# Graph layer on one Trainium2 core: the difference x[src] − x[dst] formed by an adding gather instead of a VectorE subtraction

## The chip, the cores and the metric

One core of a Trainium2 chip runs the whole program. The metric is the device time of one execution in microseconds (us); lower is better. Before the change it is 1676.12 us, the median of 3 runs (1675.56 to 1676.58).

## What is computed

`x` has 50000 rows of 512 float32. `src` and `dst` list 62500 edges, sorted by `dst`: 50000 self loops and 12500 others. Cut to what matters:

```python
msg  = x[src]
agg  = segment_sum(msg, dst, n)
deg  = segment_sum(ones, dst, n)
mean = agg / maximum(deg, 1)[:, None]
h    = mean @ W_l + b + x @ W_r
out  = layernorm(x + h * sigmoid(h))
```

Every node has its self loop, so the kernel writes mean as x[node] plus a correction, the sum of (x[src] − x[dst]) over the other edges of that node, divided by its degree. Then h = x @ (W_l + W_r) + b + correction @ W_l, and a correction is needed only for nodes that have edges other than the loop.

## The kernel before, in words

All products are float32 made of three float32r products (`three`, L484 to L491): a high and a low part of each factor, 12 matmuls of 128x512 for one tile of 128 rows. The five engine programs are written out by hand; each runs its own list of steps in order, and semaphores join them. There are three stages.

*Early stage (to about 171 us).* 44 early tiles of 128 node rows are transposed, split and multiplied by W_l + W_r; the products go to DRAM. POOL makes the low part of each early tile (`split_early`, L369 to L376), ACT the high part, a copy and the product's copy (`round_early`, `keep_early`, L629 to L641). Beside it VectorE sorts the 12500 edges out of the list (bitwise moves on `Z`, `cor`, `w_sum`) and finds node positions. Its last piece, `loop_cols` (L818 to L821), has nine rounds; `single(0, scan)` (L942) stands between round six and round seven. `upto` (L945), which PE waits for before the first edge tile, comes after round nine.

*Edge stage (173 to 527 us).* 98 tiles of 128 edges. For edge tile t:

- POOL gathers 128 rows of x by `dst` (`gather_xd`, L396) and by `src` (`gather_xs`, L400), each one indirect DMA of 256 KB, into rings of four buffers, `xd` and `xs`.
- VectorE subtracts (`subtract`, L892 to L899) into one of two `diff` buffers.
- PE turns the difference with four transposes into a PSUM buffer (`turn`, L551 to L557).
- VectorE makes running sums along equal `dst` with four scans (`scan`, L901 to L914); ACT takes the high part (`round_sums`, L660), VectorE the low part (`split_sums`, L920), PE multiplies by W_l with `three`, and VectorE scales and adds the bias (`finish`, L926). SP stores the tile as correction rows and loads `join_row`, which says where a run of equal `dst` goes on.

Orders in this stage: VectorE does, at step t, finish(t−1), scan(t+1), subtract(t+2), split_sums(t+1). PE does turn(t+1), then the 12 matmuls of tile t. ACT does round_sums(t+1). POOL issues xd(t), then xs(t); it runs ahead until the ring is full, since xd(t) waits for subtract(t−4).

Before the stage, POOL issues the gathers of tiles 0 to 3 between the early tiles 32 to 39, VectorE subtracts tiles 0 and 1 (L937, L938), and PE turns tile 0 ahead of early tile 40 (L560).

*Node stage (from 528 us).* 174 pairs of node tiles: 8 transposes, 24 matmuls, correction rows gathered and added, silu, residual, normalisation, store. The 44 early tiles are finished beside it ("light").

Of the kernel before, what the change touches and what calls it, by code (L numbers as in the profile page):

```python
# [6 lines left out]
def gnn_layer(nc, x, src, dst, w_l, w_r, bias, out):  # L7
    f32, f32r, i32 = mybir.dt.float32, mybir.dt.float32r, mybir.dt.int32
    ALU = mybir.AluOpType
    ACT = mybir.ActivationFunctionType  # L10
    P = nc.NUM_PARTITIONS

    N, D = x.shape
# [11 lines left out]
    ET = -(-R // P)  # L25
# [3 lines left out]
    EARLY = 44  # L29
    BASE = EARLY * P  # L30
    NP = -(-(NTILES - EARLY) // 2)
    MERGE_ROUND, FIND_ROUND = 4, 8
# [10 lines left out]
    with ctx:  # L43
        def sb(name, shape, dt):
            return ctx.enter_context(nc.sbuf_tensor(name, shape, dt))

        def sem(name):
            return ctx.enter_context(nc.semaphore(name))
# [3 lines left out]
        eye = eye3[:, P:2 * P]  # L52
# [30 lines left out]
        dst_idx, src_idx = sb("dst_idx", [P, ET], i32), sb("src_idx", [P, ET], i32)  # L83
        dst_f = sb("dst_f", [P, 1 + ET], f32)
        rdeg = sb("rdeg", [P, ET], f32)
        xs = [sb(f"xs{b}", [P, D], f32) for b in range(4)]
        xd = [sb(f"xd{b}", [P, D], f32) for b in range(4)]
        diff = [sb(f"diff{b}", [P, D], f32) for b in range(2)]
        join_row = sb("join_row", [P, 4, P], f32)
        sums = sb("sums", [P, 2, K, P], f32)  # L90
        s_hi = [sb(f"s_hi{b}", [P, K, P], f32r) for b in range(2)]
# [34 lines left out]
        pT = [ctx.enter_context(nc.psum_tensor(f"pT{b}", [P, 2, D], f32)) for b in range(2)]  # L126
# [26 lines left out]
        xs_in = [sem(f"xs_in{b}") for b in range(4)]  # L153
        xd_in = [sem(f"xd_in{b}") for b in range(4)]
        list_made, list_stored = sem("list_made"), sem("list_stored")
        row_in = [sem(f"row_in{b}") for b in range(4)]
        diff_made = sem("diff_made")
        turned, sums_made, s_hi_made, s_lo_made, c_product, c_made = (sem("turned"), sem("sums_made"),
                                                                     sem("s_hi_made"), sem("s_lo_made"),
                                                                     sem("c_product"), sem("c_made"))  # L160
# [25 lines left out]
        def fixed(v):  # L186
            return isinstance(v, int)

        def wait(eng, s, v):

            if not fixed(v) or v > 0:
                eng.wait_ge(s, v)
# [9 lines left out]
        def peeled(first, end, step):  # L202
            for t in range(first, end):
                step(t, t // 4, t % 4)
# [16 lines left out]
        def shifted(t, q, u, by, n, step):  # L221

            if not fixed(t) or 0 <= t + by < n:
                step(t + by, q + (u + by) // 4, (u + by) % 4)

        def single(t, step):
            step(t, t // 4, t % 4)

        def ring(q, u, n):

            return u % n, q * (4 // n) + u // n
# [120 lines left out]
        def _(pool):  # L352
            g = nc.gpsimd
# [36 lines left out]
            def gather(out_, table, idx, rows, bound, s):  # L390
                g.indirect_dma_start(out=out_, out_offset=None, in_=table,  # L391
                                     in_offset=bass.IndirectOffsetOnAxis(ap=idx, axis=0),
                                     bounds_check=bound, oob_is_err=False).then_inc(s, 16)


            def gather_xd(t, q, u):  # L396
                wait(pool, diff_made, t - 3)
                gather(xd[u][:], x, dst_idx[:, t:t + 1], P, N - 1, xd_in[u])

            def gather_xs(t, q, u):  # L400
                gather(xs[u][:], x, src_idx[:, t:t + 1], P, N - 1, xs_in[u])

            pool.wait_ge(dst_found, 1)
            for e in range(4):
                single(4 * FIND_ROUND + 2 * e, split_early)
                single(e, gather_xd)
                single(4 * FIND_ROUND + 2 * e + 1, split_early)
                single(e, gather_xs)
            peeled(4 * FIND_ROUND + 8, EARLY, split_early)
            for t in range(4, ET):  # L410
                single(t, gather_xd)
                single(t, gather_xs)

            for b in range(2):
                pool.wait_ge(c_stored[b], 16 * (ET // 2))
# [64 lines left out]
        def _(pe):  # L480
# [3 lines left out]
            def three(ps, hi, lo, w_hi, w_lo, arriving=None):  # L484

                terms = [(a, w, k) for k in range(K) for a, w in ((hi, w_hi), (hi, w_lo), (lo, w_hi))]
                for n, (a, w, k) in enumerate(terms):
                    if arriving and n % 3 == 0:
                        pe.wait_ge(arriving, k + 1)
                    last = mm(ps, a[:, k], w[:, k], start=(n == 0), stop=(n == len(terms) - 1))  # L490
                return last  # L491
# [58 lines left out]

            def turn(t, q, u):  # L551
                b = u % 2
                wait(pe, diff_made, t + 1)
                wait(pe, sums_made, t - 1)
                for k in range(K):
                    last = nc.tensor.transpose(pT[b][:, 1, k * P:(k + 1) * P], diff[b][:, k * P:(k + 1) * P], eye)
                last.then_inc(turned, 1)  # L557


            single(0, turn)  # L560
            peeled(4 * FIND_ROUND + 8, EARLY, early_tile)
            pe.wait_ge(rdeg_ready, 1)
            pe.wait_ge(upto_ready, 1)
            mm(before_ps, eye3[:, P - 1:2 * P - 1], upto[:, 1:1 + NTILES], start=True, stop=False)
# [16 lines left out]
                last.then_inc(transposed, 1)  # L581

            def edge_tile(t, q, u):
                shifted(t, q, u, 1, ET, turn)
                if fixed(t) and t == ET - 1:
                    single(0, transpose_x)
                b = u % 2
                wait(pe, s_hi_made, t + 1)
                wait(pe, s_lo_made, t + 1)
                wait(pe, c_made, t - 1)  # L590
                three(pH[b][:, 0, :], s_hi[b], s_lo[b], wl_hi, wl_lo).then_inc(c_product, 1)
            steps(pe, ET, edge_tile)


# [19 lines left out]
        def _(act):  # L614
            a_ = nc.scalar.activation
# [53 lines left out]
            def reset_light(l):  # L669
                wait(act, light_z, l)  # L670
                a_(l_cor[:], bias_rows[:], ACT.Copy).then_inc(light_reset, 1)

            peeled(EARLY - 4, EARLY, early_tile)
            single(0, round_sums)
            single(EARLY - 1, keep_early)
            act.wait_ge(bias_in, 16)
# [1 line left out]

            def edge_tile(t, q, u):
                shifted(t, q, u, 1, ET, round_sums)  # L680
                if fixed(t) and t == ET - 5:
                    act.wait_ge(idx_ready, 1)
                    reset_light(0)
                    single(0, reset_cor)
                    single(1, reset_cor)
            steps(act, ET, edge_tile)


# [58 lines left out]
        def _(dve):  # L747
            v = nc.vector
# [140 lines left out]
            dve.wait_ge(bias_in, 16)  # L889


            def subtract(t, q, u):  # L892

                b = u % 2
                r, used = ring(q, u, 4)
                dve.wait_ge(xs_in[r], 16 * (used + 1))
                dve.wait_ge(xd_in[r], 16 * (used + 1))
                wait(dve, turned, t - 1)
                v.tensor_tensor(diff[b][:], xs[r][:], xd[r][:], ALU.subtract).then_inc(diff_made, 1)  # L899

            def scan(t, q, u):  # L901

                b = u % 2
                r, used = ring(q, u, 4)
                dve.wait_ge(row_in[r], 16 * (used + 1))
                wait(dve, turned, t + 1)
                wait(dve, sums_made, t)
                wait(dve, s_lo_made, t - 1)
                wait(dve, s_hi_made, t - 1)
                for k in range(K):  # L910
                    last = v.tensor_tensor_scan(  # L911
                        sums[:, b, k], join_row[:, r], pT[b][:, 1, k * P:(k + 1) * P],
                        0.0 if fixed(t) and t == 0 else sums[:, 1 - b, k, P - 1:P], ALU.mult, ALU.add)
                last.then_inc(sums_made, 1)  # L914
# [14 lines left out]
            def find_nodes():  # L929
                dve.wait_ge(before_ready, 1)  # L930
                then(v.tensor_tensor(none, upto[:, 1:1 + NTILES], before_ps, ALU.subtract))
                then(v.tensor_scalar(none, none, 0.0, float(SKIP), ALU.is_equal, ALU.mult))
                v.memset(node_idx[:, NTILES:NTILES + 1], SKIP)
                v.scalar_tensor_tensor(node_idx[:, 0:NTILES], upto[:, 1:1 + NTILES], -1.0, none, ALU.add, ALU.add
                                       ).then_inc(idx_ready, 1)

            single(0, subtract)  # L937
            single(1, subtract)  # L938
            dve.wait_ge(loops_merged, 1)
            then(v.tensor_copy(loop_col[0], pH[1][:, 0]))  # L940
            loop_cols(0, col_bits - 3)
# [4 lines left out]
            single(0, split_sums)  # L946

            def edge_tile(t, q, u):
                shifted(t, q, u, -1, ET, finish)
                shifted(t, q, u, 1, ET, scan)  # L950
                shifted(t, q, u, 2, ET, subtract)
                shifted(t, q, u, 1, ET, split_sums)
                if fixed(t) and t == 2:
                    find_nodes()
            steps(dve, ET, edge_tile)


# [121 lines left out]
```

## Time and profile before

| | |
|---|---|
| median of 3 runs | 1676.12 us |
| the profiled execution | 1675.46 us |
| its span, first to last instruction | 1673.6 us |
| mean granted clock of TensorE | 0.993 of full |
| PE busy | 1607.3 us, 96% |
| VectorE (DVE) busy | 1446.7 us, 86% |
| ACT busy | 972.1 us, 58% |
| POOL busy | 1014.5 us, 61% |
| chain that ended last | issue 30%, PE 20%, POOL 19%, DVE 17%, ACT 10% |

Times in the rows count from the start of the span. "Idle before" is the time in which the engine did nothing ahead of an instruction, and the name behind the arrow is what ended it. Matmul ends are modelled, so PE's busy time overlaps and says less than the distance between two starts. DMA share is the mean busy share of 16 DMA engines.

### The profile page before, as it was taken

To read this page: it belongs to the slowest core of one execution; us is meant where nothing else is said; L and a number is where in the kernel's file an instruction comes from. 1 tells how busy PE (TensorE), PEld (TensorE's weight loads), DVE (VectorE), ACT (ScalarE), POOL (GpSimd) and SP (SyncE) were. 2 spreads that over 40 slices of the span, in tenths; PEclk is the share of its full clock that TensorE was granted. 3 is DMA by queue.
4 is the path that set the end of the run, shared out by engine and by line. 5 is a ranking of instruction groups with operands and counts; after the bars stand their busy time and mean duration, and the time that the engine had idled before them with its cause. 6 is when DMAs were issued, how large, how long until landed. Compare 5 with 4: busy or idle time off the path is not lost.

```text
span 1673.6 us, 30193 instructions
## 1 busy us (share of the span) xinstructions
PE 1607.3 (96%) x7886; PEld 1315.8 (79%) x7886; DVE 1446.7 (86%) x2468; ACT 972.1 (58%) x1237; POOL 1014.5 (61%) x1306
## 2 busy tenths in 40 slices
PE   7998999999999999999999999999999999999995
PEld 5887777777777788888878888887888888888884
DVE  8889999999997788888888888888888888888886
ACT  4443111111113677777767777776777777777775
POOL 5445555555553666666666666665666666666664
PEclk9999999999999999999999999999999999999998
DMA  5455788888885566666666666766666666666664
GB/s 181 150 163 173 211 238 235 238 235 236 238 233 176 159 211 224 207 218 212 211 206 217 206 223 202 224 206 200 226 198 228 203 223 211 216 207 213 209 218 162
DMA packets 204143, 349.25 MB, mean 209 GB/s; under 512 B 37020, under 2 KB 51126, under 8 KB 204117
## 3 DMA queue, kind: packets, MB, share of 16 engines
q1 hardware_dynamic: 156135, 274.22, 49.4%
q0 software_dynamic: 46944, 74.22, 17.1%
q10 hardware_dynamic: 1038, 0.50, 0.1%
q8 instruction: 11, 0.18, 0.0%
q14 instruction: 15, 0.12, 0.0%
HBM read 288.78 MB, written 139.67 MB: 256 GB/s over the span
## 4 chain that ended last, share of the span: by engine, by line
issue 30%; PE 20%; POOL 19%; DVE 17%; ACT 10%; POOLq 2%; DVEq 1%; DMA 1%; ACTq 0%; SPq 0%
PE pH L490 17%; POOL cor L391 6%; ACT O L703 4%; DVE Z L975 4%; DVE stats L990 3%; POOL rstd L462 3%; POOL light_cor L391 3%; ACT cor L666 2%; DVE sums L911 2%; POOL l_var_eps L442 2%; POOL var_eps L459 2%; ACT light_o L720 2%; DVE l_stats L1017 2%; POOL l_rstd L444 1%; ACT s_hi L660 1%
## 5 line engine op out<-in xcount | busy, mean ns | idle before, releaser
L490 PE MATMUL pH<-ws_hi,x_hi 128*128 128x512 f32 x1564 | 631.5, 404 | 13.6 <-DVE x_lo L962 6.7
L490 PE MATMUL pH<-ws_hi,x_lo 128*128 128x512 f32 x1564 | 613.3, 392 | 0.0
L490 PE MATMUL pH<-ws_lo,x_hi 128*128 128x512 f32 x1564 | 611.1, 391 | 0.0
L391 POOL DMA_INDIRECT cor<-correction_rows,node_now x347 | 370.8, 1069 | 215.4 <-POOL node_now L423 148.4
L490 PEld LDWEIGHTS pH<-ws_hi,x_hi 128*128 128x128 f32 x1564 | 295.1, 189 | 77.4 <-issue 22.7
L490 PEld LDWEIGHTS pH<-ws_hi,x_lo 128*128 128x128 f32 x1564 | 294.5, 188 | 64.5
L711 ACT ACTIVATE Z<-Z 128x1024 f32<-128x1024 f32 x174 | 184.2, 1058 | 272.2 <-DVE Z L975 236.0
L490 PEld LDWEIGHTS pH<-ws_lo,x_hi 128*128 128x128 f32 x1564 | 295.9, 189 | 55.2
L703 ACT ACTIVATE O<-Z,shift,rstd 128x512 f32<-128x512 f32 x347 | 261.5, 801 | 3.7 <-DVE shift L1001 3.7
L975 DVE TENSOR_TENSOR Z<-pH,cor 128x1024 f32<-128x1024 f32 x174 | 212.0, 1218 | 27.3 <-issue 15.2
L660 ACT ACTIVATE s_hi<-sums 128x512 fp32r<-128x512 f32 x98 | 62.0, 632 | 287.8 <-DVE sums L911 177.4
L990 DVE BATCH_NORM_STATS2 stats<-Z 128x6 f32<-128x512 f32 x347 | 221.5, 680 | 0.0
L982 DVE TENSOR_TENSOR Z<-Z,X 128x1024 f32<-128x1024 f32 x174 | 213.2, 1225 | 0.0
L962 DVE TENSOR_TENSOR x_lo<-pT,x_hi 128x1024 fp32r<-128x1024 f32 x174 | 207.3, 1191 | 2.2 <-ACT x_hi L694 2.0
L694 ACT ACTIVATE x_hi<-pT 128x1024 fp32r<-128x1024 f32 x174 | 175.2, 1007 | 36.0 <-PE pT L579 21.6
L666 ACT ACTIVATE cor<-bias_rows 128x1024 f32<-128x1024 f32 x174 | 181.5, 1044 | 0.0
L579 PEld LDWEIGHTS pT<-eye,X 128*128 128x128 f32 (+1 forms) x1388 | 161.0, 140 | 24.7 <-DMA X<-in_x 2.7
L579 PE MATMUL pT<-eye,X 128*128 128x128 f32 (+1 forms) x1388 | 179.8, 272 | 0.5 <-DMA X<-in_x 0.5
L462 POOL TENSOR_TENSOR rstd<-var_eps,minus_half 128x2 f32<-128x2 f32 x174 | 171.2, 984 | 14.5
L490 PE MATMUL pH<-wl_hi,s_hi 128*128 128x512 f32 x392 | 161.8, 413 | 15.3 <-DVE s_lo L920 5.2
L391 POOL DMA_INDIRECT xd<-in_x,dst_idx x98 | 99.3, 1014 | 122.1 <-DVE diff L899 119.5
L911 DVE TENSOR_TENSOR_SCAN sums<-join_row,sums,pT 128x128 f32<-128x128 f32 x388 | 153.8, 458 | 1.6 <-issue 1.6
(131 smaller groups left out, 1789.7 us busy)
## 6 DMA issues: line engine op xcount, KB each, us to landing
X<-in_x SPq DMA_DIRECT2D x173, 512.0 KB
out<-O SPq DMA_DIRECT2D x173, 512.0 KB
correction_rows<-c_out SPq DMA_DIRECT2D x98, 256.0 KB
light_x<-in_x SPq DMA_DIRECT2D x66, 256.0 KB
light_h<-early_product SPq DMA_DIRECT2D x44, 256.0 KB
out<-light_o SPq DMA_DIRECT2D x44, 256.0 KB
join_row<-joined SPq DMA_DIRECT2D x98, 64.0 KB
light_h<-in_x SPq DMA_DIRECT2D x22, 256.0 KB, 2.7
```

The source lines that it names most:

```text
L391: g.indirect_dma_start(out=out_, out_offset=None, in_=table, in_offset=bass.IndirectOffsetOnAxis(ap=idx, axis=0), bounds_check=bound, oob_ ...
L462: g.tensor_tensor(rstd[0:rows, b, 0:nt], var_eps[0:rows, b, 0:nt], minus_half[0:rows, 0:nt], ALU.pow).then_inc(rstd_made, 1)
L490: last = mm(ps, a[:, k], w[:, k], start=(n == 0), stop=(n == len(terms) - 1))
L579: last = nc.tensor.transpose(pT[u % 2][:, a, k * P:k * P + rows], X[0:rows, b, a, k * P:(k + 1) * P], eye[0:rows, 0:rows])
L666: a_(cor[u][:], bias_rows[:].rearrange("p (a n) -> p a n", a=1).to_broadcast([P, 2, D]), ACT.Copy).then_inc(cor_reset, 1)
L703: last = a_(O[0:rows, b, a], Z[0:rows, u % 4, a], ACT.Identity, scale=rstd[0:rows, b, a:a + 1], bias=shift[0:rows, b, a:a + 1])
L711: a_(Z[0:rows, b, 0:nt], Z[0:rows, b, 0:nt], ACT.Silu).then_inc(silu_made, 1)
L911: last = v.tensor_tensor_scan(sums[:, b, k], join_row[:, r], pT[b][:, 1, k * P:(k + 1) * P], 0.0 if fixed(t) and t == 0 else sums[:, 1 - b ...
L962: v.tensor_tensor(x_lo[b][:, 0:nt, :, 0:rows], pT[b][:, 0:nt].rearrange("p a (k r) -> p a k r", k=K)[:, :, :, 0:rows], x_hi[b][:, 0:nt, :, ...
L975: v.tensor_tensor(Z[0:rows, b, 0:nt], pH[u % 2][0:rows, 0:nt], cor[b][0:rows, 0:nt], ALU.add).then_inc(z_made, 1)
L982: v.tensor_tensor(Z[0:rows, b, 0:nt], Z[0:rows, b, 0:nt], X[0:rows, b, 0:nt], ALU.add).then_inc(u_made, 1)
L990: v.bn_stats(stats[0:rows, u % 2, a], Z[0:rows, u % 4, a]).then_inc(stats_made, 1)
```

## The change

The subtraction leaves VectorE. The gather of x[dst] goes straight into `diff`, now four buffers; ACT turns its sign in place (`negate`, Copy with scale −1); then the gather of x[src] is an indirect DMA that adds onto the same buffer. `xs` and `xd` are gone. Each adding gather waits for the sign of its tile. In POOL's list xs(t−1) now comes after xd(t), and xs(0) to xs(3) have moved behind the early tiles 40 to 43; xd(t) waits for turn(t−4). PE turns two tiles ahead of the product instead of one, waits for the adding gather to land, and turns tile 0 only after early tile 42 and tile 1 after early tile 43. VectorE does scan(t+1), finish(t−1), split_sums(t+1).

```diff
-        xs = [sb(f"xs{b}", [P, D], f32) for b in range(4)]
-        xd = [sb(f"xd{b}", [P, D], f32) for b in range(4)]
-        diff = [sb(f"diff{b}", [P, D], f32) for b in range(2)]
+        diff = [sb(f"diff{b}", [P, D], f32) for b in range(4)]
...
             def gather_xd(t, q, u):
-                wait(pool, diff_made, t - 3)
-                gather(xd[u][:], x, dst_idx[:, t:t + 1], P, N - 1, xd_in[u])
+                wait(pool, turned, t - 3)
+                gather(diff[u][:], x, dst_idx[:, t:t + 1], P, N - 1, xd_in[u])
             def gather_xs(t, q, u):
-                gather(xs[u][:], x, src_idx[:, t:t + 1], P, N - 1, xs_in[u])
+                wait(pool, negated, t + 1)
+                g.indirect_dma_start(out=diff[u][:], out_offset=None, in_=x,
+                                     in_offset=bass.IndirectOffsetOnAxis(ap=src_idx[:, t:t + 1], axis=0),
+                                     bounds_check=N - 1, compute_op=ALU.add).then_inc(xs_in[u], 16)
             for e in range(4):
                 single(4 * FIND_ROUND + 2 * e, split_early)
                 single(e, gather_xd)
                 single(4 * FIND_ROUND + 2 * e + 1, split_early)
+            for e in range(4):
+                single(4 * FIND_ROUND + 8 + e, split_early)
                 single(e, gather_xs)
-            peeled(4 * FIND_ROUND + 8, EARLY, split_early)
             for t in range(4, ET):
                 single(t, gather_xd)
-                single(t, gather_xs)
+                if t > 4:
+                    single(t - 1, gather_xs)
+            single(ET - 1, gather_xs)
...
             def turn(t, q, u):
                 b = u % 2
-                wait(pe, diff_made, t + 1)
+                r, used = ring(q, u, 4)
+                pe.wait_ge(xs_in[r], 16 * (used + 1))
                 wait(pe, sums_made, t - 1)
...
+            peeled(4 * FIND_ROUND + 8, EARLY - 1, early_tile)
             single(0, turn)
-            peeled(4 * FIND_ROUND + 8, EARLY, early_tile)
+            single(EARLY - 1, early_tile)
+            single(1, turn)
...
             def edge_tile(t, q, u):
-                shifted(t, q, u, 1, ET, turn)
+                shifted(t, q, u, 2, ET, turn)
...
-            peeled(EARLY - 4, EARLY, early_tile)
+            def negate(t, q, u):
+                act.wait_ge(xd_in[u], 16 * (ring(q, u, 4)[1] + 1))
+                a_(diff[u][:], diff[u][:], ACT.Copy, scale=-1.0).then_inc(negated, 1)
+
+            for e in range(4):
+                single(EARLY - 4 + e, early_tile)
+                single(e, negate)
...
                 shifted(t, q, u, 1, ET, round_sums)
+                shifted(t, q, u, 4, ET, negate)
...
-                v.tensor_tensor(diff[b][:], xs[r][:], xd[r][:], ALU.subtract).then_inc(diff_made, 1)
...
-            single(0, subtract)
-            single(1, subtract)
...
             def edge_tile(t, q, u):
+                shifted(t, q, u, 1, ET, scan)
                 shifted(t, q, u, -1, ET, finish)
-                shifted(t, q, u, 1, ET, scan)
-                shifted(t, q, u, 2, ET, subtract)
                 shifted(t, q, u, 1, ET, split_sums)
```

## Rows read from the trace of the kernel before

**Rows 1.** Busy time by stretch: start and end, length, then engines, clock, DMA share, GB/s.

```profile
200.00:500.00 300.00, 286.21 (x1331) 222.07 (x1330) 287.61 (x583) 52.51 (x83) 166.57 (x167) 1.00 0.84 236
700.00:1100.00 400.00, 396.41 (x1980) 329.84 (x1980) 342.90 (x574) 297.64 (x358) 261.56 (x371) 1.00 0.66 212
```

**Rows 2.** Groups of instructions in the edge stage, 200 to 500 us.

```profile
L490 PE MATMUL pH<-wl_hi,s_hi 128*128 128x512 f32 x333 | 137.5, 413 | 13.9 <-DVE s_lo L920 5.0 <-issue 4.5
L911 DVE TENSOR_TENSOR_SCAN sums<-join_row,sums,pT 128x128 f32<-128x128 f32 x333 | 132.0, 458 | 0.0
...
L391 POOL DMA_INDIRECT xd<-in_x,dst_idx x84 | 83.8, 997 | 107.6 <-DVE diff L899 106.1 <-issue 1.5
L391 POOL DMA_INDIRECT xs<-in_x,src_idx x83 | 83.4, 1005 | 27.1 <-issue 25.0 <-DVE diff L899 2.1
L926 DVE SCALAR_TENSOR_TENSOR c_out<-pH,rdeg,bias_rows 128x512 f32<-128x512 f32 x84 | 62.7, 746 | 1.2
...
L920 DVE TENSOR_TENSOR s_lo<-sums,s_hi 128x512 fp32r<-128x512 f32 x83 | 57.4, 692 | 11.2 <-ACT s_hi L660 3.9 <-issue 0.2
L899 DVE TENSOR_TENSOR diff<-xs,xd 128x512 f32<-128x512 f32 x83 | 55.3, 666 | 0.0
L660 ACT ACTIVATE s_hi<-sums 128x512 fp32r<-128x512 f32 x83 | 52.5, 633 | 247.2 <-DVE sums L911 145.6 <-issue 101.6
```

**Rows 3.** Timeline, one edge tile: start, length, engine, line.

```profile
303.49 0.69 DVE L920 TENSOR_TENSOR s_lo<-sums,s_hi 128x512 fp32r<-128x512 f32 x1
...
304.41 0.50 PE L490 MATMUL pH<-wl_hi,s_hi 128*128 128x512 f32 x1 [0.25 <-DVE s_lo L920]
```

**Rows 4.** Timeline, first matmul of edge tile 0 and of edge tile 97.

```profile
173.35 0.47 PE L490 MATMUL pH<-wl_hi,s_hi 128*128 128x512 f32 x1
...
524.31 0.47 PE L490 MATMUL pH<-wl_hi,s_hi 128*128 128x512 f32 x1
```

**Rows 5.** Groups of PE in the node stage, 700 to 1100 us.

```profile
L490 PE MATMUL pH<-ws_hi,x_hi 128*128 128x512 f32 x495 | 198.3, 401 | 3.6 <-issue 2.4
...
L579 PE MATMUL pT<-eye,X 128*128 128x128 f32 x496 | 64.3, 272 | 0.0
```

**Rows 6.** DMA queues in the edge stage, 200 to 500 us: packets, MB, share of 16 engines.

```profile
q0 software_dynamic: 13290, 43.57, 58.1%
q1 hardware_dynamic: 23931, 27.22, 26.0%
```

**Rows 7.** DMA issues: KB each and median us from issue to landing.

```profile
light_h<-in_x SPq DMA_DIRECT2D x22, 256.0 KB, 2.7
bias_rows<-in_L_gnn_b SPq DMA_DIRECT2D x1, 256.0 KB, 6.4
```

**Rows 8.** Timeline, end of the early stage and start of the edge stage.

```profile
156.00 0.60 PE L556 MATMUL pT<-eye,diff 128*128 128x128 f32 x4
...
162.34 1.35 DVE L911 TENSOR_TENSOR_SCAN sums<-join_row,pT 128x128 f32<-128x128 f32 x4
...
163.28 0.60 ACT L641 ACTIVATE light_u<-pH 128x512 f32<-128x512 f32 x1
163.47 1.30 POOL L375 TENSOR_TENSOR x_lo<-light_cor,x_hi 128x512 fp32r<-128x512 f32 x1 [3.66 <-ACT light_cor L635]
...
165.22 0.48 PE L490 MATMUL pH<-ws_hi,x_hi 128*128 128x512 f32 x1
...
167.85 0.39 PE L490 MATMUL pH<-ws_hi,x_lo 128*128 128x512 f32 x1
168.20 0.47 PE L490 MATMUL pH<-ws_hi,x_hi 128*128 128x512 f32 x1
...
171.10 0.36 DVE L945 CAST O<-Z 128x391 f32<-128x391 int32 x1
```

**Rows 9.** Busy time by stretch, the start of the node stage, columns as in rows 1.

```profile
546.00:556.00 10.00, 7.54 (x42) 6.21 (x40) 4.42 (x9) 2.91 (x5) 6.92 (x10) 1.00 0.26 78
556.00:566.00 10.00, 8.56 (x35) 6.92 (x36) 7.50 (x12) 6.24 (x9) 7.61 (x11) 0.83 0.55 181
```

More of the change, by code:

```diff
@@ L156, in gnn_layer @@
         row_in = [sem(f"row_in{b}") for b in range(4)]
-        diff_made = sem("diff_made")
+        negated = sem("negated")
         turned, sums_made, s_hi_made, s_lo_made, c_product, c_made = (sem("turned"), sem("sums_made"),
@@ L407, in _ @@
                 single(4 * FIND_ROUND + 2 * e + 1, split_early)
+            for e in range(4):
+                single(4 * FIND_ROUND + 8 + e, split_early)
                 single(e, gather_xs)
-            peeled(4 * FIND_ROUND + 8, EARLY, split_early)
+            assert EARLY == 4 * FIND_ROUND + 12
             for t in range(4, ET):
                 single(t, gather_xd)
-                single(t, gather_xs)
+                if t > 4:
+                    single(t - 1, gather_xs)
+            single(ET - 1, gather_xs)
             for b in range(2):
@@ L552, in turn @@
                 b = u % 2
-                wait(pe, diff_made, t + 1)
+                r, used = ring(q, u, 4)
+                pe.wait_ge(xs_in[r], 16 * (used + 1))
                 wait(pe, sums_made, t - 1)
                 for k in range(K):
-                    last = nc.tensor.transpose(pT[b][:, 1, k * P:(k + 1) * P], diff[b][:, k * P:(k + 1) * P], eye)
+                    last = nc.tensor.transpose(pT[b][:, 1, k * P:(k + 1) * P], diff[r][:, k * P:(k + 1) * P], eye)
                 last.then_inc(turned, 1)
+            peeled(4 * FIND_ROUND + 8, EARLY - 1, early_tile)
             single(0, turn)
-            peeled(4 * FIND_ROUND + 8, EARLY, early_tile)
+            single(EARLY - 1, early_tile)
+            single(1, turn)
             pe.wait_ge(rdeg_ready, 1)
@@ L889, in _ @@
             dve.wait_ge(bias_in, 16)
[L892 to L898, printed above, removed]
-                v.tensor_tensor(diff[b][:], xs[r][:], xd[r][:], ALU.subtract).then_inc(diff_made, 1)
             def scan(t, q, u):
```

## The prediction

> **What bounds the kernel now.** I read busy time by stretch first. In the edge stage VectorE is busy 287.6 of 300 us, PE 286.2 [rows 1]; both look full, so the groups decide. The 83 low parts in that window count 83 tiles. VectorE has 287.61 / 83 = 3.47 us of work a tile, of which the subtraction is 0.67 us, and nearly no idle time: the low part's 11.2 us in all is its largest [rows 2]. PE's busy time overlaps, so I compare spacings instead. From tile 0 to tile 97 there are 97 steps in 524.31 − 173.35 us [rows 4], 3.62 us each. In the node stage PE is busy 396 of 400 us [rows 1] and does 496 / 8 = 62 pairs [rows 5], 6.45 us a pair. A pair is 24 matmuls and 8 transposes; an edge tile asks for 12 and 4, exactly half, 3.23 us. So PE could run this loop at 3.23 and runs at 3.62; in the timeline it starts a tile when the low part has ended [rows 3]. VectorE bounds the edge stage, by its sum of work. ACT works 52.5 of 300 us there; POOL's 107.6 us before xd are waits for the subtraction [rows 2].
>
> **Removed.** 98 subtractions of 0.67 us. VectorE's work falls from 3.47 to 2.80 us a tile. PE is late next: 3.23. The scans, low part and `finish` keep their waits; since `finish` now stands between scan and low part, the 0.63 us of ACT's high part falls beside its 0.75 us [rows 2].
>
> **Signs on ACT.** 98 Copies of the high part's size, 0.63 us each [rows 2]. ACT's work becomes 1.27 us of 3.23, hidden in time in which it waits for VectorE. Behind a late sign the next high part would queue, and VectorE's low part behind that.
>
> **POOL's queue.** Two issues a tile stay, 1.00 us each with 0.33 us (27.1 / 83) between [rows 2]: 2.66 us a tile. What an adding gather costs POOL no row shows. Lower bound: the plain gather, 1.00, or a little less, which would gain nothing as POOL is then not late. Upper: two plain gathers, 2.01, as it reads two operands; that gives 3.67. Up to 1.56 is hidden under PE's 3.23. I take 1.3: nearer to one plain gather, as the list of rows is the same and written once. xd(t+2) now queues behind xs(t), so behind a sign; the ring of four gives it two steps, 6.5 us, against about 3 us until it is issued and 2.7 us to land (an estimate from a direct 256 KB load, rows 7).
>
> **The adding gather's landing.** PE reads tile t two steps after ACT's sign. The sign ends about 1.5 us into its step (two ACT instructions and their waits, an estimate from 2 × 0.63), so 2 × 3.23 − 1.5 = 5.0 us remain for issue and landing. The direct load lands in 2.7 us at the median, one at the start of the kernel took 6.4 [rows 7]. Taking 2.7 plus the 1.3 of POOL: hidden. If it is late, the turn holds up on PE the 12 matmuls queued behind it, two tiles older, and VectorE's `finish` waits for those. At 6.4 the loop would be bound by it at (1.5 + 6.4) / 2 = 3.95 us.
>
> **The DMA engines.** The queue of the gathers held them 58.1% of 300 us for 167 gathers: 1.04 us each; the other queue 26.0%, 0.94 us a tile [rows 6]. A tile takes 3.03 us of them. An adding gather has to read its target as well. Lower bound, as a plain one: 3.03. Upper, twice a plain one: 4.07. Which is nearer? The other queue moved 27.22 MB in 78 us, at which 262 KB take 0.75 us; a gather takes 1.04, just POOL's issue time, so I infer that part of it is waiting for POOL's list, which shrinks once the queue is never empty. Then the tile needs 0.75 + 1.50 + 0.94 = 3.19 us. I take this; it is so close to 3.23 that I put the loop at 3.25. **Loop: 97 × (3.62 − 3.25) = 35.9 us saved.**
>
> The Trainium skill, "Collectives: The Full Stack", section on the bandwidth ceiling, says that an add made in the DMA engine is slow not through the add but because two sources are read through the same ring, so half the rate. No run here shows it yet. By that rule the tile needs 4.07 us of the engines, and the sum would come out slower; it is the second rival.
>
> **The start.** Tile 0 is turned at 156.00 today and scanned at 162.34 [rows 8]; nothing waits there. After the change xs(1) waits for the sign of tile 1, which ACT makes after the copy at 163.28: 163.28 + 0.60 + 0.63 = 164.5. POOL issues it (1.3) and then splits early tile 42, 1.30 us, done by 167.1; today that split starts at 163.47. PE's early tile 42 starts at 167.2 instead of 165.22, takes 168.20 − 165.22 = 2.98, and turn(0) ends about 0.6 later, at 170.7. The scan of tile 0 moves from 162.34 to 170.7: **8.4 us**, and with it the three rounds behind it, `upto` (171.10, rows 8) and every edge tile, since VectorE stands still meanwhile. Lower bound: 168.20 − 162.34 = 5.9, if the splits are not late; upper 10.4, if each adding gather holds POOL 0.7 us longer three times over. PE then idles some 6 us before edge tile 0. After a similar lull in the node stage the granted clock was 0.83 in a 10 us stretch [rows 9], 1.7 us lost, so one spell at 1.2 GHz: I add 1.5, between 0 and 1.7. The two first subtractions leave 1.3 us earlier; I count nothing, they are far ahead of this wait.
>
> **Sum.** −35.9 + 8.4 + 1.5 = −26.0 on the profiled execution's 1675.46, so 1649.5; the median stands 0.66 above it: **1650 us**. Everything after 528 us is unchanged. Break-even is a loop of 3.62 − 9.9 / 97 = 3.52 us. About 0.2% (3.4 us) is what a measurement of this kernel can tell from no change.
>
> **The rivals.**
>
> 1. *POOL becomes the bound.* An adding gather of 2.01 us gives 3.67 us a tile, +4.9, with the start +9.9 and about 2 more for three longer issues: 1693, slower. It decides from 1.86 us of issue (1.66 + 1.86 = 3.52). For: two reads to describe for each row. Against: POOL's 1.00 us is steady for one list of 128 rows [rows 2].
> 2. *The DMA engines become the bound.* At 4.07 us a tile: 97 × 0.45 = +43.7, with the start +53.6: 1730, slower. It decides from 1.54 us of engine time per adding gather (3.52 − 1.04 − 0.94). A landing of 6.4 us ends near it, at 1718. For: the engines are 84% busy already [rows 1], and the add needs one more read. Against: the waiting share of a gather's 1.04 us.
> 3. *Half of it.* The adding gather costs 1.5 us of the engines and nothing shrinks: 3.48 us, 13.6 saved against 9.9: 1672, within 0.2% or just beyond.
> 4. *VectorE does not get faster.* The loop stays at 3.62 because a chain, not the sum, holds it: 1686. Against: low parts waited for ACT 3.9 us in 300 [rows 2].
>
> **How the numbers follow.** Forecast (loop 3.19 to 3.45) 0.50; rival 3 near zero 0.08; rival 1 with 4 0.17; rival 2 and beyond 0.25. Faster 0.50, same 0.08, slower 0.42. The forecast's own range is 1643 (loop 3.19, the start at 8.4 alone) to 1669 (3.45, the start at 9.9). The range of all reaches to rival 2: 1643 to 1730, leaving out landings or reads still slower (0.13) and a loop under 3.19 (0.03).
>
> **What would show it.** Right: the first matmuls of tiles 0 and 97 some 315 us apart; VectorE below 90% busy in that stretch and waiting for PE; `negate` at 0.63 us; POOL idle before xs for ACT and not the other way; scan(0) near 170.7 with VectorE idle ahead of it; node stage as before. Wrong: POOL's adding DMA_INDIRECT over 1.86 us with no idle time (rival 1); turns that wait on the DMA, with the gather queue's share over 70% (rival 2); spacing at 3.62 with VectorE idle before the low part (rival 4). The forecast falls if the step from tile to tile is above 3.52 us, whatever the start costs.

## The result, and the profile after

The changed kernel takes 1745.65 us (median of 4 runs, 1742.88 to 1750.02) against 1675.84 us for the kernel before: a ratio of 1.0418, 95% interval 1.0403 to 1.0433. It is slower by 4.2%. The prediction was 1650 us; its range of 1643 to 1730 does not reach the measured time. Its rival 2 had the direction right, at 1730, for another reason.

Nearly the whole difference lies in the edge stage and its start. Busy time by stretch of the changed kernel, the edge stage and a stretch of the node stage (columns as in rows 1: length, then PE, its weight loads, VectorE, ACT and POOL, then the clock and the DMA):

```profile
200.00:500.00 300.00, 239.15 (x1117) 183.53 (x1117) 202.04 (x419) 86.81 (x139) 182.05 (x140) 0.98 0.84 198
...
800.00:1200.00 400.00, 394.97 (x1976) 329.13 (x1975) 341.82 (x571) 296.64 (x357) 263.16 (x369) 1.00 0.65 213
```

Against [rows 1], PE fell from 286 to 239 us of 300 and VectorE from 288 to 202. No engine is full any more. The node stage is as it was. The timeline of the changed kernel: the scan of tile 0, then the first matmul of tiles 0 and 97, which answer to [rows 4, 8].

```profile
171.83 1.35 DVE L918 TENSOR_TENSOR_SCAN sums<-join_row,pT 128x128 f32<-128x128 f32 x4 [8.98 <-PE pT L563]
...
182.41 0.78 PE L496 MATMUL pH<-wl_hi,s_hi 128*128 128x512 f32 x1
...
596.29 0.48 PE L496 MATMUL pH<-wl_hi,s_hi 128*128 128x512 f32 x1
```

Tile 0 starts 182.41 − 173.35 = 9.1 us later. (In the other runs below that keep this start it lies between 180.37 and 182.71, so this term is good to 2 us.) The 97 steps take 413.9 us, 4.27 us each instead of 3.62: 62.9 us more. Together that is 72.0 of the 72.7 us by which the span grew (1746.3 against 1673.6). The groups of the edge stage say who waits (200 to 500 us, columns as in rows 2):

```profile
L400 POOL DMA_INDIRECT diff<-in_x,src_idx x70 | 107.9, 1542 | 97.2 <-ACT diff L684 87.5 <-issue 9.7
L389 POOL DMA_INDIRECT diff<-in_x,dst_idx x70 | 74.1, 1059 | 21.3 <-issue 20.7 <-PE pT L563 0.6
...
L563 PE MATMUL pT<-eye,diff 128*128 128x128 f32 x280 | 45.6, 286 | 60.8 <-DMA diff<-in_x,src_idx 60.7
...
L684 ACT ACTIVATE diff<-diff 128x512 f32<-128x512 f32 x69 | 43.5, 630 | 99.3 <-DMA diff<-in_x,dst_idx 96.2 <-issue 3.0
```

It is a circle of waits: PE's turn waits for the adding gather to land, POOL's adding gather for ACT's sign, the sign for the plain gather (xd) to land. And xd hardly waits at all: POOL issues it as soon as the adding gather ahead of it is out. The chain of waits, followed back from the last instruction and at each step to what released it, shows the circle closing. Here is one lap, and the signs that begin the next ones (start, length, what; a DMA row counts from the start of POOL's issue to the landing):

```profile
251.27 0.64 ACT diff L684
...
252.69 1.53 POOL diff L400
254.23 0.30 issue
254.53 4.62 DMA diff<-in_x,dst_idx
259.15 0.45 issue
259.60 0.64 ACT diff L684
...
267.75 0.64 ACT diff L684
...
276.33 0.64 ACT diff L684
...
285.42 0.64 ACT diff L684
```

Sign of tile t (0.64), hand-over to POOL (0.8), adding gather xs(t) (1.53), gap (0.30), then xd(t+2), which stands behind xs(t) in POOL's list and lands 4.6 us after its issue began, then the sign of tile t+2. That is 259.60 − 251.27 = 8.3 us for two tiles. The four laps from 251.27 to 285.42 take 8.2 to 9.1 us, 8.54 on average, and half of that is 4.27, the spacing measured. The landing of xd is 50.6% of the chain from 250 to 330 us, in pieces of 4.2 to 5.8 us. In between, the chain leaves the circle: from 286.85 it runs through an adding gather's landing (6.41), the turn and a product.

### The profile page after: what moved, and what is told of

It reads as the page before. It is cut to its first block, busy times and chain, and to the rows that moved or that the text cites. A ratio compares the mean times of both kernels' runs of the same rounds, so it can differ in the third digit from the quotient of the medians.

```text
span 1746.3 us, 30033 instructions
## 1 busy us (share of the span) xinstructions
PE 1609.2 (92%) x7886; PEld 1316.2 (75%) x7886; DVE 1389.8 (80%) x2370; ACT 1032.6 (59%) x1335; POOL 1073.4 (61%) x1306
## 4 chain that ended last, share of the span: by engine, by line
issue 29%; POOL 22%; DMA 14%; DVE 11%; PE 11%; ACT 10%; POOLq 2%; DVEq 1%; SPq 0%; ACTq 0%
DMA diff<-in_x,dst_idx 11%; PE pH L496 9%; POOL cor L389 6%; ACT O L719 4%; DVE Z L979 4%; POOL diff L400 3%; DVE stats L994 3%; POOL rstd L468 3%; POOL light_cor L389 2%; POOL l_var_eps L448 2%; DMA diff<-in_x,src_idx 2%; ACT cor L675 2%; POOL var_eps L465 2%; ACT light_o L736 2%; DVE l_stats L1021 2%
## 5 line engine op out<-in xcount | busy, mean ns | idle before, releaser
L400 POOL DMA_INDIRECT diff<-in_x,src_idx x98 | 151.7, 1548 | 144.1 <-ACT diff L684 121.5
```

The costliest lines, as they stand in the source:

```text
L400: g.indirect_dma_start(out=diff[u][:], out_offset=None, in_=x, in_offset=bass.IndirectOffsetOnAxis(ap=src_idx[:, t:t + 1], axis=0), bounds ...
```

## The experiments

Two theories stood first. **A:** POOL's list closes a lap of latencies over two tiles. **B:** the DMA engines are the bound, as rival 2 had it; for B spoke the DMA queues of the changed kernel in the edge stage (packets, MB, share of 16 engines), 84% in sum as in [rows 6], but for 70 tiles instead of 83:

```profile
q0 software_dynamic: 15642, 36.63, 61.1%
q1 hardware_dynamic: 20047, 22.74, 23.0%
```

Spacing below is always (first matmul of tile 97 − first matmul of tile 0) / 97, from the timeline of the run.

**One place further back in POOL's list (e2_queue3).**

```diff
-                if t > 4:
-                    single(t - 1, gather_xs)
+                if t > 5:
+                    single(t - 2, gather_xs)
```

> One line changed against the changed kernel: POOL issues xs(t-2) behind xd(t) instead of xs(t-1). Nothing else, same bytes, same adding gather. Theory A (POOL's queue closes a lap: xd(t+2) stands behind xs(t), which waits for the sign of tile t, which waits for xd(t) to land; in the chain of waits about 5.0 landing + 0.64 sign + 0.6 + 1.54 adding issue + 0.30 = 8.1 to 8.6 us for two tiles): the lap now spans three tiles, 2.8 us a tile, and the next one holds: sign, adding issue and its landing of about 5.4 us have two steps, (1.5 + 0.6 + 5.4) / 2 = 3.75 us a tile, so about 97 x 0.5 = 50 us less than the changed kernel's 1746: 1685 to 1710. Theory B (the 16 DMA engines are the bound; the adding gather takes 1.77 us of them, a tile 3.58 us at 84% busy): the order changes nothing, 1740 to 1750.

Measured: 1730.87 us, ratio 1.0313 (1.0295 to 1.0330), spacing 4.08 us. The order matters, so pure B fails, but A's price missed by 21 us. (B's 1.77 us for an adding gather is more than the rows above give: 0.611 × 300 / 70 = 2.6 us for both gathers of a tile, less 1.0 for the plain one.) The chain of waits of this run shows another lap:

```profile
260.10 0.67 PE pT L564 x4
...
261.54 1.02 POOL diff L389
262.56 0.30 issue
262.87 5.52 DMA diff<-in_x,src_idx
...
268.50 0.67 PE pT L564 x4
```

Now the adding gather of tile t−2 stands behind xd(t), which waits for the turn of tile t−4. From turn to turn it is 8.4 us, again for two tiles.

**The same, with the sign five tiles ahead (e3_queue3_sign5)** (`shifted(t, q, u, 5, ET, negate)`, and the sign of tile 4 ahead of the loop).

> As e2_queue3, and ACT turns the sign five tiles ahead instead of four. Theory A: the sign's chain has three steps now, and what is left is one lap of the ring of four: turn, xd issued and landed (5.0), sign, another xd issue in POOL (1.3), adding issue and landing (5.4), 13.8 us in all for four tiles, 3.45 us a tile, so about 80 us less than the changed kernel: 1655 to 1690. Theory B: 1740 to 1750 as before.

Measured: 1731.45 us, ratio 1.0320 (1.0294 to 1.0345), spacing 4.07. A miss by 41 us: I had counted ACT's place and overlooked the second lap, which does not go through the sign at all.

**Eight buffers, three places back (e4_ring8).**

```diff
-        diff = [sb(f"diff{b}", [P, D], f32) for b in range(4)]
+        diff = [sb(f"diff{b}", [P, D], f32) for b in range(8)]
...
-                wait(pool, turned, t - 3)
+                wait(pool, turned, t - 7)
...
-                if t > 4:
-                    single(t - 1, gather_xs)
+                if t > 6:
+                    single(t - 3, gather_xs)
...
-                shifted(t, q, u, 4, ET, negate)
+                ahead(t, q, u, 6, ET, negate)
```

(PE and ACT loop over eight tiles a turn for it; `ahead` is `shifted` for that loop; the signs of tiles 4 and 5 stand ahead of the loop.)

> Ring of eight diff buffers instead of four (PE's and ACT's loops unrolled by eight for it), POOL issues xs(t-3) behind xd(t), ACT turns the sign six tiles ahead. No latency chain is left that spans fewer than three tiles. Theory A: the loop falls to what the engines can do, PE 3.23 us a tile, the DMA engines between 3.2 and 3.5: 1650 to 1675, the start still about 9 us later than before. Theory B: 1735 to 1750, with the DMA share of the edge stage at 0.84 or more and a tile still above 4.1 us.

Measured: 1648.12 us, ratio 0.9826 (0.9810 to 0.9843). That is 2 us under A's range, and B is out. The first matmuls of tiles 0 and 97, from its timeline:

```profile
180.37 0.48 PE L511 MATMUL pH<-wl_hi,s_hi 128*128 128x512 f32 x1
...
494.20 0.48 PE L511 MATMUL pH<-wl_hi,s_hi 128*128 128x512 f32 x1
```

That is 3.235 us a tile, PE's half of a node pair (3.23) to the hundredth. From 250 to 300 us its chain of waits is PE alone (from 300 to 440 us it also runs through landings, VectorE and POOL), and its queues carry the same adding gathers at that pace:

```profile
249.95 2.75 PE pH L511 x12
252.70 0.44 PE pT L577 x4
253.14 2.75 PE pH L511 x12
```

```profile
q0 software_dynamic: 19610, 45.61, 69.0%
q1 hardware_dynamic: 27471, 32.61, 31.8%
```

The shares add up to 101%, and PE waits for landings less than 1 us of the 300. So a share near 100% does not show that the DMA engines hold the loop. POOL is another matter:

```profile
L414 POOL DMA_INDIRECT diff<-in_x,src_idx x88 | 136.3, 1549 | 28.1 <-issue 26.2 <-ACT diff L698 1.9
L403 POOL DMA_INDIRECT diff<-in_x,dst_idx x85 | 90.4, 1063 | 25.9 <-issue 11.9 <-ACT diff L698 11.0 <-PE pT L577 3.0
```

Two issues and two gaps of about 0.3 us are 1.55 + 1.06 + 0.6 = 3.2 us a tile. POOL's list is as full as PE's, and no run separates the two bounds.

**Eight buffers, and the start put back (e5_ring8_start).** Signs and adding gathers of tiles 0 to 3 go between early tiles 36 and 41, tile 0 is turned ahead of early tile 40 again. PE's part of the edit, against e4_ring8:

```diff
+            turn(0, 0, 0)
-            peeled(4 * FIND_ROUND + 8, EARLY - 1, early_tile)
-            turn(0, 0, 0)
-            single(EARLY - 1, early_tile)
+            peeled(4 * FIND_ROUND + 8, EARLY, early_tile)
             turn(1, 0, 1)
```

> As e4_ring8, and the start put back: signs and adding gathers of tiles 0 to 3 between early tiles 36 and 41, tile 0 turned ahead of early tile 40 as in the kernel before. Theory A with the start's price of 9.1 us (first matmul of tile 0 at 182.41 instead of 173.35): 8 to 10 us below e4_ring8, 1640 to 1666, so below the kernel before. If the start costs nothing in the end (something later absorbs it): the same time as e4_ring8. Theory B: about 1737.

Measured: 1642.67 us, ratio 0.9789 (0.9773 to 0.9806), the fastest of all. Its tile 0 starts here, at 174.40 instead of 180.37:

```profile
174.40 0.48 PE L511 MATMUL pH<-wl_hi,s_hi 128*128 128x512 f32 x1
```

The start gave 6.0 us at tile 0 in the trace and 5.5 in the medians, less than the 8 to 10 expected: tile 0 of e4_ring8 had already started 2.0 us ahead of the changed kernel's, and here it still starts 1.05 us behind the kernel before.

**Is it the ring or the order (e6_ring8_near)?** The two laps can be written down. With n buffers and xs(t) standing d places behind, xd(t+d+1) waits behind xs(t): a lap of d+1 tiles. And xs(t) waits behind xd(t+d), which waits for the turn of tile t+d−n: a lap of n−d tiles. With n = 4 one of them always spans two tiles, for d = 1 as for d = 2. This is theory A2. Eight buffers with d = 1 (`t - 1` again):

> As e4_ring8 (eight buffers, 3.24 us a tile), but POOL issues xs(t-1) behind xd(t) again, as the changed kernel does. Theory A2 (two laps through POOL's list: xd(t+d+1) stands behind xs(t), d+1 tiles a lap; xs(t) stands behind xd(t+d), which waits for turn(t+d-n), n-d tiles a lap; each lap is some 8.1 to 8.6 us; with d = 1 the first spans two tiles whatever the ring): about 4.1 to 4.3 us a tile, 1730 to 1750, as if the ring were still four. Rival C (it is the number of buffers that counts, or the loops unrolled by eight): 1645 to 1652 as e4_ring8.

Measured: 1778.63 us, ratio 1.0590 (1.0563 to 1.0616), spacing 4.61. C is out: eight buffers alone gain nothing. But 29 us over the range needs a reason. The groups show it:

```profile
L943 DVE TENSOR_TENSOR s_lo<-sums,s_hi 128x512 fp32r<-128x512 f32 x65 | 45.0, 692 | 108.2 <-ACT s_hi L683 107.0
```

In the changed kernel this row waits for nothing (0.0 us). Here ACT waits 222.1 of 300 us at signs six tiles ahead whose gathers have not landed, and the high part queues behind them. To test that, the same kernel with the sign four ahead (e9_ring8_near_sign4; the signs of tiles 4 and 5 ahead of the loop go too):

```diff
-                ahead(t, q, u, 6, ET, negate)
+                ahead(t, q, u, 4, ET, negate)
```

> As e6_ring8_near (eight buffers, xs(t-1) behind xd(t)), with ACT turning the sign four tiles ahead as in the changed kernel, instead of six. Against the changed kernel only the ring and the loops unrolled by eight differ. e6_ring8_near took 4.61 us a tile, more than the 4.3 expected, with VectorE's low part waiting 107 of 300 us for ACT's high part, which stands behind a sign that waits for its gather. Theory A2 (the lap through POOL's list spans two tiles whatever the ring, and the excess in e6_ring8_near is ACT's line behind the early sign): 4.2 to 4.3 us a tile as in the changed kernel, 1738 to 1752. If the excess comes from eight buffers or from the unrolled loops: 1770 to 1785 again. If the ring is what counted: under 1700.

Measured: 1747.19 us, ratio 1.0436 (1.0418 to 1.0454), spacing 4.25, the changed kernel's 4.27 with eight buffers. VectorE's low part waits for nothing again:

```profile
L941 DVE TENSOR_TENSOR s_lo<-sums,s_hi 128x512 fp32r<-128x512 f32 x71 | 48.4, 682 | 0.0
```

Buffers and unrolled loops are worth nothing while d is 1.

**Two places back with eight buffers (e7_ring8_mid)** (laps of three and six tiles).

> As e4_ring8, with xs(t-2) behind xd(t). Theory A2: laps of three and of six tiles, 8.4 / 3 = 2.8 us, so PE still holds the loop at 3.24: 1645 to 1652. If the lap in this setting is longer because landings are (5.6 us instead of 5.0 in e4_ring8), 9.2 / 3 = 3.07, still under 3.24. Rival C: the same time; rival D (the lap grows with every tile of distance lost): 1690 or so.

Measured: 1651.91 us, ratio 0.9850 (0.9834 to 0.9867), spacing 3.27. The time is at the upper end of A2's range. But from 250 to 300 us the chain of waits runs through landings and POOL's issues and not through PE, and ACT waits 172.5 us for landings, against 14.8 in e4_ring8: the laps priced at 2.8 to 3.1 us a tile seem to leave little in reserve.

**The sign taken out of the lap (e8_no_sign).** POOL waits for xd's landing itself (the four signs ahead of the loop go too):

```diff
-                wait(pool, negated, t + 1)
+                pool.wait_ge(xd_in[u], 16 * (ring(q, u, 4)[1] + 1))
...
-                shifted(t, q, u, 4, ET, negate)
```

> The changed kernel without the sign: ACT's negate is left out and POOL's adding gather waits for the landing of xd itself, so the output is made of x[src] + x[dst]. Same order, ring and adding gather. Theory A2: the lap loses the sign's 0.64 us and one hand-over of about 0.5 us, 8.5 - 1.2 = 7.3 us for two tiles, 3.65 a tile, so 97 x 0.6 = 58 below the changed kernel: 1680 to 1700. Theory B (the DMA engines' capacity): the same DMA work, 1740 to 1750.

Measured: 1720.66 us (2 runs), ratio 1.0260 (1.0233 to 1.0287), spacing 4.00. Faster than the changed kernel by 25 us with the same DMA work, so it is a latency; but 21 us above the range. One lap of its chain:

```profile
253.39 1.54 POOL diff L400
254.93 0.30 issue
255.23 5.49 DMA diff<-in_x,dst_idx
...
261.50 1.54 POOL diff L400
```

From 255.23 + 5.49 to 261.50 POOL's hand-over still takes 0.8 us: 1.54 + 0.30 + 5.49 + 0.8 = 8.1 for two tiles, 4.05 a tile. The sign's 0.64 us is gone, but the hand-over of 0.5 that the expectation took off is not, and the landings in this stretch of the chain, to 300 us, are 5.4 us and more.

**The adding taken out (e1_plain_second).**

```diff
-                                     bounds_check=N - 1, compute_op=ALU.add).then_inc(xs_in[u], 16)
+                                     bounds_check=N - 1).then_inc(xs_in[u], 16)
```

> The changed kernel with a plain second gather, which overwrites where the other adds, so x[dst] is left out of the result. Same order, waits, ring and sign. Theory A2: the lap loses 0.54 us of POOL's issue (1.54 to 1.00) and perhaps 0.5 to 0.9 us of xd's landing, which queues behind the adding gather: 7.1 to 7.8 us for two tiles, 3.55 to 3.9 a tile, 1680 to 1710: most of the loss stays without any adding. If the adding in the DMA engines is the cause: 3.24 to 3.4 a tile and 1650 to 1665.

Measured: 1707.33 us (2 runs), ratio 1.0181 (1.0160 to 1.0201), spacing 3.82. POOL's second issue is back to 1.04 us:

```profile
L400 POOL DMA_INDIRECT diff<-in_x,src_idx x78 | 81.3, 1042 | 110.0 <-ACT diff L684 71.9 <-issue 19.8 <-PE pT L563 18.4
```

With two plain gathers and the same order the kernel is still 30 us slower than the kernel before. Against PE's 3.24 the changed kernel loses 1.03 us a tile; 0.58 of it stays without any adding, and 0.45 goes with it. The split of the 0.45 is an estimate: 0.50 us a lap is the longer issue, and the landings of xd on the chain of waits from 200 to 475 us average 5.2 us in the changed kernel (27 of them) and 4.7 here (20).

## Why the prediction was wrong, point by point

- *What bounds the kernel now; VectorE's sum; PE next at 3.23.* Right, with POOL level with PE. With eight buffers the loop ran at 3.235 us, and the time was 1648 us where 1650 had been forecast for a loop at 3.25.
- *Signs on ACT, 0.63 us.* Right in size: 630 ns in the group. Hidden as work, yes, but part of a lap.
- *POOL's queue.* The failed step is here, and it is the size of one term. The paragraph says that xd(t+2) queues behind xs(t), "so behind a sign", and sets two steps, 6.5 us, against about 3 us until xd(t+2) is issued and 2.7 us for it to land. Those two terms are the circle: xs(t), xd(t+2), landing, sign, xs(t+2). Until the issue the lap shown takes 0.64 + 0.8 + 1.53 + 0.30 = 3.3 us, near the 3 taken. The landing, counted from the start of its issue, takes 4.2 to 5.8 us instead of 2.7, so the lap is 8.54 and not under 6.5. Two things hid it. The sum was read as slack, with no time of its own should it come out longer, though a circle sets a pace: its length over its tiles. And the two steps were put down to the ring of four; they come from the order of the list, since eight buffers in the same order gave 4.25. The issue itself was priced within its bounds: 1.3 taken, 1.54 measured, 0.02 under the 1.56 that PE hides.
- *The landing's source.* 2.7 us came from a direct load. With it the lap would have been about 6 us, 3.0 a tile, and hidden. The bound of 6.4 stood beside it, but was carried into the adding gather's landing alone, not into xd's, where 3 + 6.4 us for two tiles would have been 4.7 a tile. No row of the kernel before shows such a landing. Its trace has one of an indirect gather, 2.7 us (issued at 535.05, VectorE released at 537.77), but in a stretch where that queue moved only 0.18 MB in 5 us. The Trainium skill, "DMA: Bandwidth & Descriptors", section "Anatomy of one DMA — SWDGE (gpsimd) path", gives 2.0 us and the bytes at 436 GB/s, an estimate of 2.6 us for 256 KB; the landings in the edge stage do not agree, and the measurement decides.
- *The adding gather's landing.* Priced at 1.3 + 2.7 = 4.0 us of the 5.0 left, and hidden. PE's turns waited 60.7 of 300 us for it in the changed kernel; how much of that is its own length and how much the late issue in the circle, no run separates. Where it lies on the chain from 200 to 475 us it takes 5.9 to 6.7 us from the start of its issue, and 4.6 to 5.9 with the list one place further back.
- *The DMA engines.* Priced at 3.19 to 4.07 us a tile and put beside the loop as if a bound. They did not hold the changed kernel: with the same adding gathers the loop ran at 3.235. The rule of the Trainium skill, "Collectives: The Full Stack", section on the bandwidth ceiling, on two reads is seen in part. A pair of gathers held the queue 0.611 × 300 / 70 = 2.62 us with the add and 0.506 × 300 / 78 = 1.95 without (its share was 50.6% for 78 pairs in the run without the adding), so there an adding gather took about 1.6 us and a plain one 1.0, not twice. With eight buffers a pair took less, 0.690 × 300 / 87 = 2.38 us (45.61 MB are 87 pairs), so 1.4 for the adding gather; the prediction's 1.50 lies between. What it would make of the kernel's time, 4.07 us a tile, did not come.
- *The start.* 8.4 + 1.5 priced; 9.1 measured at tile 0, the scan at 171.83 where 170.7 was given, and the clock fell as feared, in busy time by stretch of the changed kernel ahead of and at tile 0:

```profile
170.00:178.00 8.00, 5.13 (x26) 3.87 (x24) 5.90 (x13) 2.35 (x4) 5.41 (x5) 0.98 0.60 129
178.00:184.40 6.40, 5.45 (x13) 3.72 (x14) 5.11 (x13) 1.15 (x2) 1.43 (x1) 0.50 0.29 99
```

  PE was busy 5.1 of 8 us and idle for the last 3.8 before 178.95, then its granted clock was 0.50, the lower level of 1.2 GHz; the first matmul of tile 0 took 0.78 us instead of 0.47 [rows 4]. Undoing the new start gave 5.5 us.
- *Rival 2* had the sign of the result and nearly its size for a reason that the runs exclude. Its sign, a gather queue over 70%, misleads: 61.1% in the changed kernel, 69.0% in the fast e4_ring8. Rival 1 is out, as POOL's adding issue averages 1.54 us, under the 1.86 where it decides, and POOL idles 97 us before it. Rival 4 is out, as VectorE's work did fall, to 202.04 / 70 = 2.89 us a tile, and the loop then ran at 3.235. Rival 3's loop of 3.48 is 0.8 us short of the measured one.

What stays open: why a gather takes 4 us and more to land when its rows occupy the engines about 1 us. No run separated POOL's issue, the queue and the signal that the last row has landed. And the landings counted are those on the chain of waits, so rather the late ones.

## What to carry to other kernels

A queue that issues in order turns a new wait into an edge of a graph: for every instruction that waits, ask what stands behind it in its queue and follow that until it comes back to the same instruction some tiles later. The sum of the latencies round that circle, divided by the tiles that it spans, is a bound just like an engine's work; adding buffers helps only the circles that pass through the ring, and moving the waiting instruction further back trades one circle for another unless the ring grows too. Price an indirect gather's landing from an indirect gather of as many bytes in a stretch as busy, and where no row shows it, carry the far bound through every place in which it stands.

## What was not expected of the hardware

- Indirect gathers of 128 rows of 2 KB, where they lay on the chain of waits of the changed kernel from 250 to 330 us, landed 4.2 to 5.8 us after the start of their issue, an adding one after 6.4, with the engines busy 84% by their share.
- An adding gather cost POOL 1.54 us in the changed kernel (1.74 on average in e6_ring8_near) against 1.00 to 1.13 for a plain one, and 0.4 to 0.7 us more of the DMA engines.
- The DMA share reached 1.01 over 300 us, with PE's turns and products still back to back; a share of 0.84 was the same for a kernel that was bound by VectorE and for one that was bound by a lap.
